# A fused state-space convolution and FP4 feed-forward kernel: the second gate product moved ahead of the h transposition and the first convolution group

## The reference

```python
xn = _layernorm(x, axis=-1)
s = _L0_attn_ref(xn, ...)        # causal convolution with 128 taps per channel, + xn * D
g = _silu(_L0_ffn_ref(xn, ...))  # FP4-quantised gated feed-forward
x = x + s * g

def fp4_quant_dequant(x):        # blocks of 16 along the last axis
    scale = jnp.maximum(jnp.max(jnp.abs(xb), axis=-1, keepdims=True) / 6.0, 1e-12)
    idx = jnp.searchsorted(_MID, jnp.abs(xb / scale))
    return _GRID[idx] * jnp.sign(xb / scale) * scale
gate = fp4_linear(x, w_gate)     # 256 -> 704, both operands quantised
y = fp4_linear(x, w_up)          # 256 -> 704
h = jax.nn.silu(gate) * y
return fp4_linear(h, w_down)     # 704 -> 256, h quantised too
```

## Time and profile before

| | |
|---|---|
| median of 3 runs | 653.93 us (650.7 to 657.33) |
| the profiled execution | 651.98 us, span 650.2 us |
| TensorE busy | 492.9 us (76%) |
| VectorE busy | 574.4 us (88%) |
| ScalarE busy | 403.6 us (62%) |
| GpSimd busy | 218.2 us (34%) |
| chain that ended last, by engine | TensorE 41%, VectorE 30%, DMA 11% (of which 10% the loads of `kpad`) |
| mean granted TensorE clock | 0.966 |

### The profile page before, as it was taken

The page is one execution under the profiler, slowest core; times in us unless marked ns, Lnnn a source line. Parts: engine busy times, 40 slices in busy tenths (PEclk is TensorE's granted clock), DMA queues, the critical chain, the costliest instruction groups (busy, mean ns, idle before and its releaser), DMA issues.

```text
span 650.2 us, 13028 instructions
## 1 busy us (share of the span) xinstructions
PE 492.9 (76%) x4856; PEld 339.3 (52%) x4856; DVE 574.4 (88%) x688; ACT 403.6 (62%) x562; POOL 218.2 (34%) x304
## 2 busy tenths in 40 slices
PE   0000057757978889999999999999999888788872
PEld 0000045424555557777676777767676555455552
DVE  6999999889999999999988898888898989787792
ACT  7960088675888886666666666666666656455551
POOL 1138720044444453111111132222121464773512
PEclk9999997697999999999999999999999989889997
DMA  6950000221424215555555555545553364731424
GB/s 194 348 180 0 0 1 16 82 83 22 148 84 153 89 50 144 152 167 149 153 147 147 147 147 146 147 146 147 147 146 83 54 95 74 108 61 26 72 33 66
DMA packets 101026, 70.80 MB, mean 109 GB/s; under 512 B 8944, under 2 KB 100592, under 8 KB 100848
## 3 DMA queue, kind: packets, MB, share of 16 engines
q1 hardware_dynamic: 92512, 61.68, 31.9%
q0 software_dynamic: 8464, 8.39, 9.4%
HBM read 61.28 MB, written 17.17 MB: 121 GB/s over the span
## 4 chain that ended last, share of the span: by engine, by line
PE 41%; DVE 30%; DMA 11%; issue 7%; POOL 6%; ACT 3%; SPq 0%; ACTq 0%; DVEq 0%; POOLq 0%
PE ps L1190 16%; DMA work<-kpad 10%; PE ps L1208 9%; PE ps L1210 5%; DVE work L839 4%; PE ps L1199 3%; DVE wgu L926 3%; PE ps L1223 3%; PE ps L1227 3%; DVE work L834 3%; ACT work L618 2%; DVE work L873 2%; POOL gbuf L493 2%; POOL out L497 2%; PE ps L1178 2%
## 5 line engine op out<-in xcount | busy, mean ns | idle before, releaser
L1190 PE MATMUL ps<-wgu,work 128*128 128x512 f16 (+1 forms) x1152 | 243.9, 367 | 7.8 <-DVE work L865 6.6
L1190 PEld LDWEIGHTS ps<-wgu,work 128*128 128x128 f16 x1152 | 112.5, 99 | 117.5 <-issue 9.9
L603 ACT ACTIVATE work<-ps,con 128x704 f32<-128x704 f32 x64 | 54.2, 847 | 118.0 <-PE ps L1190 118.0
L598 ACT COPY work<-ps 128x1408 f16<-128x1408 f16 x64 | 84.9, 1327 | 20.8 <-PE ps L1199 20.5
L1208 PE MATMUL ps<-wdh,work 128*128 128x256 f16 x704 | 90.1, 278 | 2.5 <-ACT work L598 1.9
L834 DVE SCALAR_TENSOR_TENSOR work<-work 128x960 f32<-128x960 bf16 (+2 forms) x67 | 74.7, 1116 | 18.1 <-ACT work L618 18.0
L1199 PE MATMUL ps<-id,work 128*128 128x128 f16 x704 | 50.5, 221 | 38.8 <-DVE work L873 29.1
L493 POOL TENSOR_TENSOR gbuf<-gbuf,xh 128x512 f32<-128x512 f32 x28 | 40.1, 1442 | 106.7 <-DVE work L847 97.1
L865 DVE TENSOR_TENSOR work<-work,ps 128x704 f32<-128x704 f32 x64 | 56.5, 882 | 20.6 <-ACT work L603 20.5
L1208 PEld LDWEIGHTS ps<-wdh,work 128*128 128x128 f16 x704 | 67.3, 99 | 10.8 <-ACT work L598 2.0
L839 DVE SCALAR_TENSOR_TENSOR work<-work 128x1920 f16<-128x1920 bf16 (+3 forms) x36 | 69.8, 1938 | 1.2
(11 more groups left out here) (151 smaller groups left out, 764.9 us busy)
## 6 DMA issues: line engine op xcount, KB each, us to landing
work<-kpad SPq DMA_DIRECT2D x64, 512.0 KB, 4.6
gbuf<-u_rev SPq DMA_DIRECT2D x4, 2048.0 KB, 18.4
work<-L_attn_u SPq DMA_DIRECT2D x32, 256.0 KB, 4.2
out<-gbuf POOLq DMA_DIRECT2D x15, 512.0 KB, 6.3
work<-L_ffn_w_down SPq DMA_DIRECT2D x1, 704.0 KB, 7.0
work<-L_ffn_w_gate SPq DMA_DIRECT2D x1, 640.0 KB, 4.5
work<-L_ffn_w_up SPq DMA_DIRECT2D x1, 640.0 KB, 5.8
out<-gbuf POOLq DMA_DIRECT2D x1, 384.0 KB, 5.1
```

Of the source, the lines that this page charges most:

```text
L598: nc.scalar.copy(hT[par], src).then_inc(hT_a, 1)
L1190: last = T.matmul(p_gu[:, a:b], xT[par][:, t, c, :], wgu[:, part, c % 2, a:b], start=(n == 0), stop=(n == len(todo) - 1))
```

## The change

TensorE: `gate_up` of tile `m + 1` moves from behind `h_transpose(it * 2 - 3, ...)` to directly behind `down(it * 2 - 4, 0)`. In steps without convolution it passes one `h_transpose`; in convolution steps it passes the first and the second `conv` call too. The first `h_transpose` of a step gets a wait on `x_tc`. ScalarE: the two squares stand in a row with the copy of x behind them, and `silu_gate` of tile `m + 1` moves ahead of the second `h_copy` (and of `a_high`). No instruction is added or removed on either engine; VectorE, GpSimd and SyncE have the same order as before.

```diff
--- before.py
+++ after.py
@@ -643,10 +643,10 @@
                 if gu:
                     silu_gate(it * 2)
                 square(it, 1 - par, x, ch, 0)
+                if ch:
+                    square(it, 1 - par, x, ch, 1)
                 if xt:
                     x_copy(it + 1, 1 - par)
-                if ch:
-                    square(it, 1 - par, x, ch, 1)
                 if xn:
                     x_norm(it + 3, 1 - par)
                 if td:
@@ -655,13 +655,13 @@
                     silu_out(it * 2 - 4, 0, par)
                 if cv:
                     y_copy(it * 2 - 2 * S_CONV)
+                if gu:
+                    silu_gate(it * 2 + 1)
                 if td:
                     h_copy(it * 2 - 3, 1)
                 if a2:
                     a_high(it * 2, it + (NT // 8 + 1))
                     a_high(it * 2 + 1, it + (NT // 8 + 1))
-                if gu:
-                    silu_gate(it * 2 + 1)
                 if ch:
                     down_scale(it - 1, 1 - par)
                 if cv:
@@ -1230,7 +1230,7 @@
             def step(it, par, x, gu, td, cv=False):
                 if td:
                     pe.wait_ge(hl_v, it - 1)
-                    h_transpose(it * 2 - 4, 0, par)
+                    h_transpose(it * 2 - 4, 0, par, copied=min(it + 1, NP))
                     if it > 2:
                         down(it * 2 - 5, 1)
                 if gu:
@@ -1239,14 +1239,14 @@
                     x_transpose(it + 1, 1 - par)
                 if td:
                     down(it * 2 - 4, 0)
+                if gu:
+                    gate_up(it * 2 + 1, 1, par, None)
                 if cv:
                     pe.wait_ge(a_lp, NT // 4)
                     conv(it * 2 - 2 * S_CONV, 0)
                     conv(it * 2 - 2 * S_CONV, 1)
                 if td:
                     h_transpose(it * 2 - 3, 1, par, copied=it + 2 if x else None)
-                if gu:
-                    gate_up(it * 2 + 1, 1, par, None)
                 if cv:
                     conv(it * 2 - 2 * S_CONV + 1, 0)
                     conv(it * 2 - 2 * S_CONV + 1, 1)
```

## The result

The changed kernel takes 734.75 us (median of 4 runs, 731.94 to 736.68) against 653.32 for the kernel before, measured beside it: a ratio of 1.123, 95% interval 1.118 to 1.128. The profiled execution took 731.94 us, with a span of 730.2, so 80.0 us more span than before. The forecast was 721 us, the range 702 to 744. The kernel before was measured again beside each group of experiments (medians 654.2, 655.83 and 655.12 us), so totals from different groups can differ by up to 2.5 us for that alone. In the group without loads one execution of the changed order (1835 us) and two of the kernel before (1028 and 1346 us) stand far above all others and are not in the ratios.

The account below looks back on a forecast made before the run. It took VectorE as busiest before the convolution and TensorE as the bound in it. From the profiled 651.98 us: 651.98 - 3.9 - 2.0 + 62.4 + 12 = 720.5, say 721 us, range 702 to 744.

Parts of the forecast that it names:

- Part 2, the loads: Convolution steps: gate product no longer covers the fourth call's filter load; TensorE idles 4.2 us a step, stage 62.4 us more.
- Part 3, the clock: Convolution steps: granted clock falls once a step after the load gap; 0.75 of 1.67 us counted, 12 us in all.
- Part 1, the squares: Both squares in a row end VectorE's 0.65 us wait: 3.9 us gained before the convolution, 2.0 us after, none in it.
- "I cost it at nothing", the moved silu: ScalarE in convolution steps: silu ahead delays the copy of h by 0.85 us; counted as nothing, at most 0.85 a step.
- The clock that holds: Convolution steps: the filter transfer is late but the granted clock stays full, 708.5 us; chance 0.15.
- The rival of the full clock price: Convolution steps: clock falls cost in full, 15 us more, or landings are slow; up to 747 us; chance 0.15.
- slow landings: Convolution filter loads land in 5.8 instead of 5.1 us, 11 us more; chance 0.15, shared with the full clock price.
- The copy out of PSUM: Third convolution call waits for ScalarE's copy, not the load: 0.3 us a step, 646 us in all; chance 0.03.
- The hidden transfer: Third and fourth convolution calls: the load stays hidden, steps of 15.56 us, kernel 641 us; chance 0.03.
- The signs: Profile after: filter waits above 60 us, convolution steps 19 to 21 us, one clock fall each, earlier steps 14.4 to 14.5.
- The likeliest case's own range: Whole kernel around 721 us: landings of 4.8 to 5.4 us and clock price 0.4 to 1.3 us a step, 707 to 735.

Follow-up runs that it names:

- the group without loads: All filter loads but the first two left out: 654.33 us in the changed order, 642.57 us in the order of the kernel before.
- the filled kernel: Changed kernel plus 24 extra TensorE products ahead of the third convolution call and 4 ahead of the fourth: 711.09 us, ratio 1.087.

## Why the prediction was right, point by point

- **Part 2, the loads.** Right in mechanism, and near in size. The interval from the second to the fourth call is 6.17 us in the mean (forecast 6.25), since the load for the fourth call lands after 5.1 us as before. With the 13.34 us of the rest of a step at full clock that makes 19.51 us (forecast 19.8). The stage's term is (19.51 - 15.97) x 16 = 56.6 us, against 62.4. Without loads the loss is gone, and it goes too with the gate product behind the calls.
- **Part 3, the clock.** One fall a step was right; its price was not, and this is the term that was mis-sized. It was taken as 0.75 us a step, 12 us; it measures 1.73 a step, 27.7 us. The reason given for 0.75, that part of the slow time lies under the wait for the fourth call, did not hold: in the step shown the clock falls 0.2 us before the fourth call, and that call, the transpositions and the down products pay. Besides, in five of the 16 steps the clock stayed at half for twice as long, which no row of before had shown. The full price of one fall, 1.67 us, was the better figure (1.6 in the filled kernel); the measured sum lies just above the upper end that was given, 27.
- **Part 1, the squares.** Right for one step: 14.4 instead of 15.1 us, and VectorE's wait is gone. Of the 3.9 us ahead of the convolution 1.7 came. The last five steps there give 3.3 us, but 1.6 had been lost before they begin, 1.0 of it in one step that takes 15.89 us instead of 14.92. VectorE waits 1.30 us in it for the first silu, and the clock is at half from 161.1 us, just before that step. That this is its cause is argued, not shown. Behind the convolution 2.7 us came, against 2.0, but by other steps than counted: they differ from before by anything from -1.7 to +0.7 us, so this agreement is partly luck. In the order before, the same edit is worth 7 us by the medians, with hardly any of it ahead of the convolution.
- **"I cost it at nothing", the moved silu.** No wait for the copy of h is seen in the convolution step shown of the changed kernel. Without the loads the order costs about 1 us a step; which part of it is the silu's was not separated.
- **The rivals.** The clock that holds was priced at 708.5 us, and the filled kernel, in which it nearly does, takes 711; without filling, the clock fell. The rival of the full clock price was right on that half: with 27 us for the clock and nothing else changed the forecast's sum would be 735.5. The other half, slow landings, did not come. The copy out of PSUM exists, at 0.41 us, and shows only without loads. The hidden transfer did not occur: landings in the step shown were 4.3 and 5.2 us.
- **The signs.** The waits for the filter block reached 59.1 us, where above 60 was forecast, and the steps 21.24 us, just over the 19 to 21. The likeliest case's own range was also added up a little wide: its terms give 710 at the low end, not 707.
- **The sum.** 651.98 + 56.6 + 27.7 - 1.7 - 2.7 = 731.9, the profiled execution. The forecast of 720.5 missed it by 11: the clock is 15.7 us more and the squares won 1.5 less, while the loads cost 5.8 less. The two large errors have opposite signs, so the total came nearer than its clock term deserved. Had the loads cost what was forecast, the kernel would have taken about 738 us, still inside the range.

## What to carry to other kernels

Ask of every step that is moved what it stood in front of: a gate product of 3.7 us that looked like plain work was the cover of a transfer of 5 us behind a two-deep buffer. Measure the distance from a buffer's release to its next use as work between them, and compare it with issue plus landing. When TensorE has slack, where its idle lies may matter too: here 2.4 us in one piece brought falls of the clock that 2.3 us in two pieces had not. And when a run is used to price one effect, check that the others stayed the same in it: the filled kernel's loads landed 0.3 us later, and the plain difference of the two kernels hid a third of what the falls cost.

## What the runs showed of the hardware

Ahead of the convolution, two idles of 0.5 and 1.76 us a step left the clock at full level; one idle of 2.4 us a step brought it to half (1.2 of 2.4 GHz) in most steps, and the kernel lost 12 to 14 us; filled down to 1.56 us it stayed at full. In the changed kernel's convolution steps a wait on the load of 3.2 us (in the step shown), one call and a wait of 0.7 us brought a fall of the clock in each of 16 steps; a fall cost 1.6 us in the filled kernel. Extra products in that gap made the kernel 24 us faster. A filter load of half the bytes landed in 3.5 instead of 4.2 us in the median, and in 3.9 instead of 5.1 as the second of two issued 0.7 us apart.
